# Nine of the sixteen token tiles' stream mixing moved from VectorE to GpSimd

## The reference, cut to what matters

```python
H_res = sinkhorn_log(H_res_logits)              # [B, T, 4, 4]
H_res = (1.0 - g) * I + g * H_res
x_pre = jnp.einsum('btnc,btn->btc', x_streams, H_pre)
y = x_pre @ W_branch
x_mixed = jnp.einsum('btij,btjc->btic', H_res, x_streams)
y_distributed = jnp.einsum('btc,btn->btnc', y, H_post)
return (x_mixed + y_distributed).reshape(B, T, nC)
...
x = x + attention(xn) + ffn(xn)                  # layer 0; then layer norm, and layer 1
```

## Time and profile before

| | |
|---|---|
| time of the profiled execution | 2586.59 us |
| its span (first to last instruction) | 2584.8 us |
| mean granted clock of PE | 0.952 |
| DVE busy over the span | 1561.2 us (60%), 3304 instructions |
| POOL busy over the span | 891.9 us (35%), 931 instructions |
| PE busy over the span | 2336.5 us (90%), 11994 instructions |
| layer0_mix after `mix_ok` | 252 to 378.4 us |

### The profile page before, as it was taken

How to read it: one execution, slowest core, us unless ns; L and a number is a source line. 1 busy time by engine, 2 the same in 40 slices (tenths; PEclk the granted TensorE clock), 3 DMA queues, 4 the chain that set the end, 5 groups by cost and what they waited for, 6 DMA issues and landing times.

```text
span 2584.8 us, 37835 instructions
## 1 busy us (share of the span) xinstructions
PE 2336.5 (90%) x11994; PEld 1873.0 (72%) x11994; DVE 1561.2 (60%) x3304; ACT 1087.2 (42%) x2259; POOL 891.9 (35%) x931
## 2 busy tenths in 40 slices
PE   5754767569889999999999999999999999999998
PEld 4642326458678888888888888888878888888886
DVE  3489983544546656565655656565665656565665
ACT  3342322024434445454444445454444445444443
POOL 2755001000133525253343525253342515243331
PEclk9866887879999999999999999999999999999999
DMA  2175010117820110101010112201010110101010
GB/s 83 38 282 205 1 28 1 66 49 245 286 71 24 42 49 16 49 24 57 8 57 24 41 49 81 81 24 57 8 57 30 35 49 21 56 12 57 8 45 29
DMA packets 99935, 158.00 MB, mean 61 GB/s; under 512 B 10232, under 2 KB 45816, under 8 KB 97712
## 3 DMA queue, kind: packets, MB, share of 16 engines
q1 hardware_dynamic: 97760, 154.20, 17.7%
q0 software_dynamic: 544, 2.10, 0.2%
q10 hardware_dynamic: 1584, 1.11, 0.1%
HBM read 98.67 MB, written 58.72 MB: 61 GB/s over the span
## 4 chain that ended last, share of the span: by engine, by line
PE 67%; DVE 2%; ACT 2%; issue 1%; ACTq 0%
PE psum L51 20%; PE psum L53 18%; PE psum L52 18%; PE psum L1614 9%; DVE pT L1519 2%; ACT pT L1560 1%; PE psum L1603 1%; DVE oT L1523 0%; ACT oT L1564 0%; ACT probs L1554 0%; DVE q L1495 0%; DVE acc L1527 0%; ACT q L1544 0%; ACTq L1559 0%; DVE nmax L1505 0%
## 5 line engine op out<-in xcount | busy, mean ns | idle before, releaser
L1483 POOL TENSOR_TENSOR probs<-probs,rinv 128x1024 f32<-128x1024 f32 (+7 forms) x384 | 439.1, 1147 | 1109.4 <-DVE rinv L1510 1109.4
L1519 DVE TENSOR_TENSOR pT<-psum,pT 128x512 fp32r<-128x512 f32 x576 | 387.2, 689 | 312.8 <-ACT pT L1560 307.4
L1554 ACT ACTIVATE probs<-psum,nmax 128x256 f32<-128x256 f32 (+7 forms) x512 | 380.9, 744 | 365.0 <-DVE nmax L1505 360.5
L1560 ACT ACTIVATE pT<-psum 128x512 fp32r<-128x512 f32 x576 | 330.3, 595 | 332.1 <-PE psum L1614 331.1
L1505 DVE TENSOR_REDUCE nmax<-psum 128x1 f32<-128x256 f32 (+7 forms) x512 | 378.3, 752 | 44.6 <-PE psum L1603 38.4
L1614 PE MATMUL psum<-ident,probs 128*128 128x128 f32 x2304 | 329.3, 273 | 5.2 <-issue 3.1
L1614 PEld LDWEIGHTS psum<-ident,probs 128*128 128x128 f32 x2304 | 262.7, 141 | 44.4 <-DVE pT L1519 8.9
L51 PE MATMUL psum<-keys,q 128*128 128x512 f32 (+3 forms) x768 | 276.7, 360 | 1.4 <-DVE q L1495 1.4
L51 PE MATMUL psum<-pT,vals 128*128 128x512 f32 x576 | 263.5, 457 | 3.9
L53 PE MATMUL psum<-keys,q 128*128 128x512 f32 (+3 forms) x768 | 261.8, 341 | 0.0
L52 PE MATMUL psum<-keys,q 128*128 128x512 f32 (+3 forms) x768 | 261.4, 340 | 0.0
(11 more groups left out here) (280 smaller groups left out, 4033.7 us busy)
## 6 DMA issues: line engine op xcount, KB each, us to landing
vals<-v_parts SPq DMA_DIRECT2D x32, 512.0 KB, 4.2
xT<-wq_parts SPq DMA_DIRECT2D x15, 1024.0 KB, 5.3
keys<-k_parts SPq DMA_DIRECT2D x30, 512.0 KB
xT<-wo_parts SPq DMA_DIRECT2D x15, 1024.0 KB, 5.3
wraw<-in_L_attn_Wq SPq DMA_DIRECT2D x8, 1024.0 KB, 7.2
wraw<-in_L_attn_Wo SPq DMA_DIRECT2D x8, 1024.0 KB, 7.5
wq_parts<-wturned SPq DMA_DIRECT2D x8, 1024.0 KB, 5.0
wo_parts<-wturned SPq DMA_DIRECT2D x8, 1024.0 KB, 5.4
```

What stands on the lines that cost most here:

```text
L1483: pool.tensor_tensor(p, p, rinv[:, u, h:h + 1].to_broadcast([P, (TB - u) * P]), ALU.mult).then_inc(p_ok, 1)
L1519: dve.tensor_tensor(pT[:, n % PT_SLOTS, 1, :], bank[T_BANK + n % 2], f32(pT[:, n % PT_SLOTS, 0, :]), ALU.subtract).then_inc(t_lo, 1)
L1554: act.activation(probs[:, u % 2, h, 0:n], bank2[2 * (h % 2)][:, off:off + n], ACT.Exp, bias=nmax[:, u, h:h + 1], accum_out=rsum[:, u, h:h ...
L1560: act.activation(pT[:, n % PT_SLOTS, 0, :], bank[T_BANK + n % 2], ACT.Copy).then_inc(t_hi, 1)
```

## The change

POOL does the four `xn` terms of tiles 7 to 15 (`MIX_POOL` = 9) after its Sinkhorn loop. For each tile and each source stream j it does two instructions of 128x512: a multiplication of the stream, repeated over the four output streams, by the column j of the matrix, into a new buffer `mixing`; and the addition of `mixing` to `x1[t]`. Each waits for the one before it (`pool_mixed`), 72 instructions in all. DVE keeps all five terms of tiles 0 to 6 and the `y` terms of tiles 7 to 15, which now stand at the end of its list. `last_op` of the nine tiles points at POOL's semaphore, so DVE waits for POOL before it touches such a tile.

```diff
+        MIX_POOL = 9
+        mixing = sb("mixing", [P, NS, D])
...
+            pool.wait_ge(mix_ok, 1)
+            n = 0
+            for t in range(NT - MIX_POOL, NT):
+                x = x1[:, t, :].rearrange("p (i c) -> p i c", i=NS)
+                for j in range(NS):
+                    if n:
+                        pool.wait_ge(pool_mixed, n)
+                    stream = xn[:, t, j * D:(j + 1) * D].unsqueeze(1).to_broadcast([P, NS, D])
+                    pool.tensor_tensor(mixing[:], stream, T[:, t, :, j].unsqueeze(2).to_broadcast([P, NS, D]),
+                                       ALU.mult).then_inc(pool_mixed, 1)
+                    pool.wait_ge(pool_mixed, n + 1)
+                    pool.tensor_tensor(x, x, mixing[:], ALU.add).then_inc(pool_mixed, 1)
+                    n += 2
...
-            last_op = {t: (mix_ok, 1) for t in range(NT)}
+            last_op = {t: (mix_ok, 1) for t in range(NT - MIX_POOL)}
+            last_op.update({NT - MIX_POOL + k: (pool_mixed, 2 * NS * (k + 1)) for k in range(MIX_POOL)})
...
-            terms = [(t, j) for k in range(0, NT, 2) for j in range(NS + 1) for t in (k, k + 1)]
+            own = range(NT - MIX_POOL)
+            terms = [(t, j) for k in range(0, len(own), 2) for j in range(NS + 1) for t in own[k:k + 2]]
+            terms += [(t, NS) for t in range(NT - MIX_POOL, NT)]
```

More of the change, by code:

```diff
@@ L375, in layer0_mix @@
         t_mm, t_ok, pv_mm = (sem("b_" + n) for n in ("tmm", "t", "pv"))
-        o_ok, wo_mm, x1_ok, mixed = (sem("b_" + n) for n in ("o", "womm", "x1", "mixed"))
+        o_ok, wo_mm, x1_ok, mixed, pool_mixed = (sem("b_" + n) for n in ("o", "womm", "x1", "mixed", "poolmixed"))
         RW_STEPS, HEAD_STEPS = 5, 11
```

## The result

The changed kernel takes 2618.27 us (median of 4, 2617.7 to 2619.09; three more executions gave 2614.55, 2616.7 and 2618.44 us); the kernel before, with one more run beside it, 2588.03 us. The ratio is 1.0116, 95% interval 1.0102 to 1.0131: slower by 30 us. Forecast were 2619 us and slower.

A forecast was written before the change was run, and what follows sets the result against it. DVE, one mixing instruction passing per POOL instruction, was taken to bound units 0 and 1, then PE. 47.2 us lost less 14.9 won back gave +32.3 on 2586.6, say 2619 us (+1.25%); range 2594 to 2640.

The forecast's parts named there:

- What bounds the stage: After the Sinkhorn loop DVE, busy 42.23 of 42.5 us, sets the block's end at 378.39 us.
- That GpSimd's reads hold VectorE instructions with two SBUF inputs: Units 0 and 1: a mixing instruction waits for the POOL instruction under way to end, some 1.2 us instead of 0.35.
- the sign given: Mixing instructions between 254 and 341 us should last 0.9 to 1.3 us, ending about 0.2 us after a POOL start.
- One passes per POOL instruction, and POOL isn't slowed: Units 0 and 1: one mixing instruction per POOL instruction of 1.245 us; a group of 8 takes 11.2 us.
- The claim at 0.20 us and the next request at 0.262: After release, POOL claims the inputs at 0.20 us, before DVE's next mixing instruction could begin at 0.262.
- POOL's 89.5 us: POOL's 36 pairs at 2.49 us each, from 252.0 to 341.5; bounds 81 and 99 us.
- Units 0 and 1: Eight groups of mixing instructions use all 72 POOL instructions; unit 1's terms end at 341.6 instead of 294.4, +47.2 us.
- The way back: From the third unit PE bounds: scores after 3.8 us, two units of 23.8, then 11.9 and 5.8; end 410.7.
- The sum: Block end: 47.2 us lost and 14.9 won back give 410.7 against 378.4, +32.3 us; 2619 us.
- Two per POOL instruction: Rival for units 0 and 1: two mixing instructions pass, POOL's are 0.19 us late; +12 us, 2599; chance 0.15.
- VectorE keeping the inputs: Rival: DVE keeps the inputs while mixing instructions are queued, POOL stretches to 376; +4 us, 2590; chance 0.08.
- No holding at all: Rival: mixing instructions beside POOL are hardly held and stay at 0.35 us; -24.2 us, 2562; chance 0.10.

The follow-up runs named there:

- e1_left_out: Changed kernel with POOL's 72 mixing instructions left out and nothing in their place (tiles 7 to 15 lack the four xn terms); 2558.19 us.
- e2: Changed kernel with POOL's 72 instructions replaced by 72 memsets of 128x1024, which write SBUF and read nothing; 2552.88 us.
- e3: Changed kernel with POOL's same 72 instructions and waits on buffers of its own that no other engine touches; 2616.32 us.
- e8: Changed kernel with a memset of 128x1 on POOL, waited for on both sides, between every two of its 72 instructions; 2593.79 us.
- e4: Changed kernel with POOL's products issued one ahead of its additions, in three buffers, so none waits for the one right before it; 2609.39 us.
- v8: Kernel before, with ScalarE making all y products ahead of the Sinkhorn loop's end and some xn products, nothing on GpSimd; 2577.10 us, ratio 0.9966.

## Why the prediction was right, point by point

**What bounds the stage.** VectorE, as read: with 144 of its instructions gone and nothing added (e1_left_out) the stage falls to 95.5 us.

**That GpSimd's reads hold VectorE instructions with two SBUF inputs.** The step on which all depended, drawn from three DVE instructions beside POOL, and for the three-operand form only expected. It holds for that form: 330 to 1433 ns, long only beside POOL's two-input instructions. e2 and e3 narrow it to those, whatever the addresses. The held ones took up to 1.43 us where 0.9 to 1.3 was the sign given, and ended 0.07 us after POOL's next start instead of 0.2: that figure came from a POOL that didn't wait and so started 0.12 us sooner after its forerunner. The distance that counts, from POOL's end, is 0.15 us. The rule of the Trainium skill (SBUF — State Buffer, "Who interferes with whom") that a GpSimd instruction that only writes doesn't contend is borne out by e2 (346 ns beside memsets).

**One passes per POOL instruction, and POOL isn't slowed.** 64 instructions went through beside 72 of POOL, whose medians, 1047 and 1262 ns, are within 0.02 us of the 1.04 and 1.28 of the earlier trace rows. The eight intervals in which none passed lie one ahead of each group of eight, where VectorE does a maximum. The claim at 0.20 us and the next request at 0.262 were a margin of 0.06 worked out from differences of records; e8 moved the one past the other and got two (as inferred above), e4 moved it the other way and delayed POOL by 0.04.

**POOL's 89.5 us.** Measured 88.7, from 248.4 to 337.1. The estimate of 85.7 us by the cycles per element of the Trainium skill (GPSIMD Engine Reference, "Elementwise — side-by-side cycle accounting") is not what the trace shows.

**Units 0 and 1.** 89.6 us forecast, 88.9 measured to the first addition.

**The way back.** Forecast 69.1 us from there to the end, measured 66.5 (337.26 to 403.74). The term mis-sized is the stretch from the projections to the next scores, taken as 5.1 us from the unit at 319.08, in which VectorE had still been late with its additions. With VectorE on time it is 3.79 (360.88 to 364.67, and again 383.37 to 387.16), and the last stretch 4.74 instead of 5.8. That makes 3.7 us too many; 1.1 us were lost elsewhere, since PE starts the third unit slowly: its first scores take 2.44 us instead of 1.88, and come 4.35 us after the first addition instead of 3.8. The granted clock was 0.66 from 338 to 345 us, after a stretch (300 to 337 us) in which PE was busy for 12.7 of 37 us, and 1.00 from 345 on. The prediction had named this for its range, with up to 4 us, and put it at nothing in the sum. The stage came to 155.4 instead of 158.7.

**The sum.** Stage +29.0 instead of +32.3; the remaining microsecond or two of the measured difference lie outside the stage, in what differs from run to run. That the forecast met the time within 1 us is in part luck: the stage was forecast 3.3 us too long, the kernel before measured 1.4 us higher than in the runs I had, and the rest lies outside the stage.

**Rivals.** Two per POOL instruction: not in this kernel, but what e8 shows with a gap 0.18 us wider, and then 2594 (2599 was worked out for it). VectorE keeping the inputs: no run shows it; POOL went between any two held instructions. No holding at all: out; its price was too small, -24 against the -31 us of e1's stage. The 5.1 us stood in it three times and the last stretch once, 5.0 us too many. The remaining 1.7 are an error in its working: it added the 18.7 us of a unit counted from the scores to a start at the transposes (L692), which come 1.7 us later (283.53 and 285.24 in e1).

## What to carry to other kernels

Before work goes from VectorE to an idle GpSimd, look at what VectorE will run beside it. If its instructions have two inputs in SBUF and GpSimd's read SBUF, each waits for a whole GpSimd instruction, and then the count of VectorE's instructions sets the time, not their size: 0.35 us became 1.2 to 1.4. Give such work to ScalarE if it has the time (v8 gained 0.3%), or keep GpSimd beside VectorE instructions that read PSUM: the maxima kept to 1.21 us.

One SBUF input is no safe sign by itself. Layer 1 of the kernel before has VectorE instructions (L1515) that scale one SBUF tile by a number per partition. The smallest is the slower one of these two groups (columns: busy us, mean ns | idle before):

```profile
L1515 DVE TENSOR_SCALAR probs<-probs,rinv 128x128 f32<-128x128 f32 x16 | 7.5, 466 | 0.6
...
L1515 DVE TENSOR_SCALAR probs<-probs,rinv 128x256 f32<-128x256 f32 x16 | 5.6, 353 | 0.6
```

All 16 of 128x128 ran beside a GpSimd instruction and ended 0.08 us after it; none of the 16 of 128x256 did. At 128x640, where both cases occur, it is 0.67 us beside GpSimd (15) and 0.55 without (1). No run tests the cause there, but the rows are warning enough. The reductions (L507), also with one SBUF input, ended before the GpSimd instruction beside them did and so weren't held by it. So read the holding off an earlier place of the same trace, form by form, by comparing one form's duration with the other engine quiet and busy.

## What the runs showed of the hardware that was not expected

- More work on GpSimd can make the kernel faster: a 0.1 us memset between its instructions let two VectorE instructions pass instead of one and cut the stage by 22 us (155.4 to 133.1). It is still longer than the 126.4 of the kernel before.
- A ScalarE product of 128x128 from SBUF with a per-partition scale took 0.396 us, eight in a row 2.46 us, so 0.31 each; four of them cost more than VectorE's 4 x 0.262.
- PE's projections of a unit take 3.8 us to the next scores when VectorE is on time, 1.3 us less than any unit of the kernel before had shown.
